# Two layers of cross-attention and expert layers on one core: stacked queries and keys kept in DRAM in the order of the tiles that load them

## The chip, the cores and the metric

One core of one Trainium2 chip. The metric is the device time of one execution in microseconds (us); the profile adds one execution recorded by the hardware. TensorE is PE in the rows (PEld its weight loads), VectorE DVE, ScalarE ACT, GpSimd POOL, and SP is the engine that does nothing here but wait and issue transfers; a row with SPq is the time that one issue took on it, not the transfer's.

## The reference, cut to what matters

Sixteen batches of 256 tokens of width 256 attend to 77 context rows each, twice, with an expert layer behind each attention. The change lies in the first attention alone, with 16 heads of 16 numbers:

```python
qh = (q @ Wq.T + bq).reshape(B, QN, H, DH).transpose(0, 2, 1, 3)
kh = (k @ Wk.T + bk).reshape(B, KN, H, DH).transpose(0, 2, 1, 3)
vh = (v @ Wv.T + bv).reshape(B, KN, H, DH).transpose(0, 2, 1, 3)
qh = layernorm(qh, q_gamma, q_beta) * scale
kh = layernorm(kh, k_gamma, k_beta)
attn = jax.nn.softmax(jnp.einsum('bhqd,bhkd->bhqk', qh, kh), axis=-1)
x = jnp.einsum('bhqk,bhkd->bhqd', attn, vh)
```

## The kernel before, in words

The program is a chain of stages with a barrier behind each: queries, keys and values of all batches (`qkv_phase`, from the start to about 151 us of the profiled span), the first attention (`attention0_phase`, about 151 to 395 us), routing and experts, the second attention, routing and experts, the last sum. Only the first two are touched.

**First stage.** A piece is two batches of keys (8 pieces, class `HeadNorm` as `k`) or 256 rows of x, which is one batch of queries (16 pieces, `q`). Each piece is projected on PE, normalised over the 16 numbers of a head on ACT and DVE, transposed on PE into one PSUM bank (`transpose`, L231), then scaled and shifted on ACT into two copies in SBUF, `full` in float32 and `high` in the rounded type float32r (`affine`, L242; the activations are L249). POOL takes `low` as the difference of the two (`part`, L252). SP stores high and low to DRAM (`store`, L258, issued at L264): a piece of keys in 2 transfers, a piece of queries in 8 of 32 rows each. Buffers of `high` and `low` are double: `affine` of piece i waits until the stores of piece i-2 have landed (L246). All engines walk through steps; SP's step (L384) loads the x rows of a later piece, stores the piece that is four steps behind, and at four steps (`PRELOAD`) loads the stacked queries and keys of batches 0 to 3. The stage ends when every engine has issued its last instruction.

**Stacked operands.** For the first attention a batch's queries and keys lie in SBUF with 96 rows: queries as high, high, low, keys as high, low, high (32 rows each, two heads of 16), so that one matmul over 96 rows gives the product to nearly full precision. The keys of a pair of heads stand in two column blocks, the other head's 16 rows being zero; POOL zeroes the four key buffers once at the start (L411). `load_queries_keys` (L283) fills them with nine transfers: three for the queries (32 rows of 8 KB each), six for the keys (16 rows of 8 runs of 308 bytes each). There are four buffers (`QK_RING`), so batch b+4 is loaded when batch b is done with.

**First attention.** It runs in half-steps u of 128 queries by 8 heads; the work of one (scores, maxima, exponentials, values, projection, layer norm, router) is spread over the 21 half-steps from u on. At half-step u: PE computes scores (L886) and DVE reduces them to maxima (L774, so that row marks the half-steps: 64 of them, u = 0 at 152.15 us); every second one the maxima are transposed, copied by ACT (L848) and sent by SP into rows 96 and 97 of the query buffer in two transfers (L679), from where the second score product (L900) takes them three half-steps later. Beside that, the first expert weights are loaded (L665, 1 MB every eight half-steps, at u = 5, 13, ...) and split into high and low in 64 chunks: ACT copies a chunk (L856), POOL subtracts (L748) into one of four tiles `low`, SP stores it (L699). SP takes all this in one program order per half-step (`half`, L672): maxima, expert weights, next batch of queries and keys (at u = 9, 13, ..., 53, after the second score product of half-step u-1), input rows, chunk of low, two result rows. At u = 12 it issues twelve loads for later stages in a row (L714, L718).

Of the kernel before, what the change touches and what calls it, by code (L numbers as in the profile page):

```python
# [12 lines left out]
ALU = mybir.AluOpType  # L13
# [151 lines left out]
class HeadNorm:  # L165
# [4 lines left out]
    def __init__(self, sb, sem, g, name, rows, w, ones, bias, gamma, beta, eps, ps_p, ps_t, parts, stored, store_rows):  # L170
# [4 lines left out]
        n = 2 * DC * rows  # L175
        at = [parts[:, i * n:(i + 1) * n] for i in range(6)]
        self.full, self.high, self.low = at[0:2], *([a.bitcast(F32R) for a in at[i:i + 2]] for i in (2, 4))
        self.stored, self.store_rows = stored, store_rows
        self.landed = 2 * len(store_rows) * 16
# [51 lines left out]
    def transpose(self, pe, i):  # L231
        p, r = i.mod(2), self.rows
        pe.wait_ge(self.s_n, i.n + 1)

        wait(pe, self.s_out, i.n)
        for a in range(2):
            for c in range(DC):
                last = pe.transpose(self.ps_t[:, (c * 2 + a) * r:(c * 2 + a + 1) * r],
                                    self.n[p][0:r, (a * DC + c) * P:(a * DC + c + 1) * P], self.g.ident[0:r, 0:r])
        last.then_inc(self.s_t, 1)  # L240

    def affine(self, act, i, s_passed):  # L242

        p, n = i.mod(2), 2 * DC * self.rows
        wait(act, self.s_low, i.shift(-1).n)
        wait(act, self.st[p], i.div(2).n * self.landed)  # L246
# [22 lines left out]
Q_ROWS = [(i * 2 * DH, (i + 1) * 2 * DH) for i in range(P // (2 * DH))]  # L269
Q_STORES = 2 * len(Q_ROWS)  # L270


def query_rows(part):

    return lambda b, first, last: part.rearrange("r b (c m) t -> m r b c t", c=DC)[first // (2 * DH)][:, b, :, :]


def key_rows(part):

    return lambda i, first, last: part.rearrange("(c p) k -> p c k", p=P)[:, :, i * 2 * LK:(i + 1) * 2 * LK]  # L280


def load_queries_keys(sp, g, b, slot):  # L283

    landed = g.s_qk[slot]
    for j, part in enumerate((0, 0, 1)):
        sp.dma_start(g.q3[slot][32 * j:32 * j + 32, :].bitcast(F32).rearrange("p (h t) -> p h t", h=HG),
                     g.q_parts[part][:, b, :, :]).then_inc(landed, 16)
    for j, part in enumerate((0, 1, 0)):
        for a in range(2):  # L290
            at = 32 * j + DH * a
            sp.dma_start(
                g.k3[slot][at:at + DH, :].bitcast(F32).rearrange("p (h a k) -> p h a k", h=HG, a=2)[:, :, a, :],
                g.k_parts[part].rearrange("(h a p) k -> a p h k", a=2, p=DH)[a][:, :, b * LK:(b + 1) * LK])\
                .then_inc(landed, 16)


def qkv_phase(nc, g):

    ctx = ExitStack()  # L300
    with ctx:
        def sb(name, shape, dt=F32):
# [10 lines left out]
        wmean, bmean = sb("wmean", [P, 2, DC * H]), sb("bmean", [2 * H, 1])  # L313
        gb, scaled, eps, bv = sb("gb", [P, 4]), sb("scaled", [P, 2]), sb("eps", [P, 1]), sb("bv", [P, 2 * D])
# [5 lines left out]
        k_split = g.w2[:, 4 * D + 12 * 2 * P:4 * D + 12 * 2 * P + 12 * 2 * LK]  # L320
# [11 lines left out]
        g.s_qk, s_neg, s_zero = [sem(f"s_qk{i}") for i in range(QK_RING)], sem("s_neg"), sem("s_zero")  # L332
        neg = g.w2[:, 6 * W2_COLS:6 * W2_COLS + HG * 2 * LK]
        ps_p, ps_t, ps_xt, ps_v = g.bank[0:4], g.bank[4], g.bank[5:7], g.bank[7]
        k = HeadNorm(sb, sem, g, "k", LK, wk, ones3, bias3[:, 0:D], gb[:, 2:3], gb[:, 3:4], eps, ps_p, ps_t,
                     k_split, [key_rows(part) for part in g.k_parts], [(0, P)])
        q = HeadNorm(sb, sem, g, "q", P, wq, ones3, bias3[:, D:2 * D], scaled[:, 0:1], scaled[:, 1:2], eps, ps_p, ps_t,
                     q_split, [query_rows(part) for part in g.q_parts], Q_ROWS)
# [24 lines left out]
        def _(sp):  # L363
            sp.dma_start(bias[:, :], g.ins["bkq"].rearrange("o (h d) -> (o h) d", d=DH)).then_inc(s_b, 16)
            sp.dma_start(wk[:, :], g.ins["wk"]).then_inc(s_wk, 16)
            for dst, src in ((wv, g.ins["wv"]), (gb, g.ins["gb"]), (bv, g.ins["bv"]), (g.ident, g.ins["ident"])):
# [17 lines left out]
            def step(s):  # L384
# [5 lines left out]
                if s.off in PRELOAD:  # L390
                    b = PRELOAD.index(s.off)
                    if b == 0:
                        sp.wait_ge(s_zero, QK_RING)
                        for st in k.st:
                            sp.wait_ge(st, NKP // 2 * k.landed)
                    sp.wait_ge(q.st[b % 2], (b // 2 + 1) * q.landed)
# [5 lines left out]
        def _(pool):  # L402
# [7 lines left out]
            for slot in range(QK_RING):  # L410
                pool.memset(g.k3[slot][0:96, :].bitcast(F32), 0.0).then_inc(s_zero, 1)  # L411
# [13 lines left out]
        def _(dve):  # L425
# [21 lines left out]
            dve.wait_ge(s_rest, 4 * 16)  # L447
            dve.tensor_scalar(scaled[:, :], gb[:, 0:2], float(DH) ** -0.5, None, ALU.mult).then_inc(s_gs, 1)
            dve.wait_ge(s_v1, 1)
# [36 lines left out]
        def _(act):  # L486
# [6 lines left out]
            act.wait_ge(s_gs, 1)  # L493
# [18 lines left out]
        def _(pe):  # L512
# [13 lines left out]
            def step(s):  # L526
# [8 lines left out]
                if (at := piece(s, 0)) is not None:  # L535
                    norm, i = at
                    if norm is k:
                        if i.off == 0:
                            pe.wait_ge(s_rest, 4 * 16)
# [25 lines left out]
def attention0_phase(nc, g):  # L565
# [3 lines left out]
    with ctx:  # L569
# [33 lines left out]
        low_st = [sem(f"low_st{i}") for i in range(4)]  # L603
# [54 lines left out]
        def _(sp):  # L658
# [12 lines left out]

            def half(u):  # L672
                m = max_rows(u)
                if m is not None:
                    sp.wait_ge(mt_out, m.n + 1)
                    b, gr = m.div(2), m.mod(2)
                    n = HG // 2 * SQ
                    for a in range(2):
# [1888 lines left out]
```

## Time and profile before

| | |
|---|---|
| median of 3 runs | 1444.58 us (1439.33 to 1449.13) |
| profiled execution | 1436.91 us, span of its instructions 1435.1 us |
| busy share of the span | PE 89%, DVE 58%, POOL 51%, ACT 45% |
| first stage | 0 to 151 us |
| first attention | 151 to about 395 us |

Read it by stages: a busy share over the whole span says little on the two stages in question. Where an engine sits idle, the row says in brackets for how long and what ended the wait. A row on transfers gives packets (the pieces into which a transfer is cut, one contiguous run each, and its small packets), bytes, and the share of 16 transfer engines' time that the packets took.

### The profile page before, as it was taken

The page shows a single profiled execution, that of the slowest core. Times are in us where ns is not written, and L with a number is a line of the kernel's source. Part 1 is how long each engine was busy: PE and PEld are TensorE (multiplying, and loading weights), DVE is VectorE, ACT ScalarE, POOL GpSimd, SP SyncE. Part 2 cuts the span into 40 slices and gives each one's busy share as a digit, 9 for nine tenths or more (in the row PEclk, how much of TensorE's full clock was granted, in tenths as well). Part 3 has the DMA queues.
Part 4 walks back from the last instruction along what each step waited for, and adds up shares of the span by engine and source line. Part 5 has one row for each costly group of instructions (what it writes and reads, how often), then busy time and mean ns, then how long its engine had stood idle before and what let it go on. Part 6 is the DMA issues. An engine that isn't in the chain of part 4 may idle for free. (4 is left out here: it accounts for less than half of the span.)

```text
span 1435.1 us, 27993 instructions
## 1 busy us (share of the span) xinstructions
PE 1270.8 (89%) x7093; PEld 995.2 (69%) x7094; DVE 838.1 (58%) x2027; ACT 648.6 (45%) x1350; POOL 728.7 (51%) x963
## 2 busy tenths in 40 slices
PE   7876779999887999999999499847999999969997
PEld 4554447667655888888888377624888888857776
DVE  5753236556584777777777588694333333346665
ACT  3544347767523545455554277635433333321110
POOL 2332236566502565555655366404655555267775
PEclk9986579999998999999999699957999999989999
DMA  3487486885352556555555588554555556774443
GB/s 105 115 197 159 132 224 193 234 216 173 123 236 87 172 156 164 165 158 171 155 170 147 183 255 226 158 234 148 174 162 161 162 161 157 136 226 131 129 134 115
DMA packets 157086, 240.44 MB, mean 168 GB/s; under 512 B 34812, under 2 KB 122125, under 8 KB 152144
## 3 DMA queue, kind: packets, MB, share of 16 engines
q1 hardware_dynamic: 134584, 173.48, 41.8%
q0 software_dynamic: 20640, 56.39, 14.1%
q10 hardware_dynamic: 1784, 9.66, 1.7%
q8 instruction: 33, 0.54, 0.2%
q14 instruction: 45, 0.37, 0.1%
HBM read 164.41 MB, written 70.55 MB: 164 GB/s over the span
## 5 line engine op out<-in xcount | busy, mean ns | idle before, releaser
L1346 POOL DMA_INDIRECT xg<-t_xn,token x160 | 151.3, 945 | 156.8 <-PE psum L2246 69.2
L2322 POOL DMA_INDIRECT su_yg<-t_y,slot x128 | 122.9, 960 | 67.5 <-issue 38.7
L2258 PE MATMUL psum<-gu,m_xT 128*128 x640 | 153.2, 383 | 0.0
L2217 DVE TENSOR_TENSOR m_h<-psum,m_sg 128x256 f32<-128x256 f32 x80 | 34.0, 425 | 158.7 <-ACT m_sg L2196 158.7
L2258 PEld LDWEIGHTS psum<-gu,m_xT 128*128 128x128 f32 x640 | 116.6, 192 | 12.9
L1599 PE MATMUL psum<-w,m_xT_high 128*128 x284 | 118.6, 418 | 0.0
L1621 PE MATMUL psum<-m_both,m_hT_high 128*128 128x512 f32 x284 | 111.3, 414 | 1.4 <-DVE top_i L1565 1.2
L1599 PE MATMUL psum<-w_low,m_xT_high 128*128 x284 | 112.3, 396 | 0.0
L1599 PE MATMUL psum<-w,m_xT_low 128*128 x284 | 112.3, 395 | 0.0
L1472 POOL DMA_INDIRECT t_y<-top_v,dest x36 | 67.7, 1880 | 69.3 <-DVE top_v L1565 66.9
L1546 DVE TENSOR_TENSOR m_both<-w,m_both 128x1024 fp32r<-128x1024 f32 x71 | 87.0, 1225 | 17.2 <-ACT m_both L1514 17.1
L1472 POOL DMA_INDIRECT t_y<-top_i,dest x35 | 62.0, 1771 | 62.8 <-DVE top_i L1565 54.6
L833 ACT ACTIVATE at_prT<-psum 77x1024 f32<-77x1024 f32 x64 | 65.3, 1020 | 60.2 <-PE psum L900 60.1
L1337 POOL DMA_INDIRECT xg<-t_xn,token x54 | 52.6, 973 | 73.0 <-POOLq L1355 51.8
L1521 ACT ACTIVATE m_h<-psum 128x512 f32<-128x512 f32 x71 | 42.4, 598 | 103.6 <-PE psum L1599 103.6
L1551 DVE TENSOR_TENSOR m_h<-psum,m_h 128x512 f32<-128x512 f32 x71 | 49.1, 691 | 61.2 <-ACT m_h L1521 61.2
L2279 PE MATMUL psum<-dn,m_hT 128*128 x320 | 82.6, 381 | 1.7 <-DVE m_y L2225 1.7
L774 DVE TENSOR_REDUCE at_mx<-psum 128x8 f32<-128x616 f32 x64 | 51.2, 800 | 51.6 <-PE psum L886 51.1
L2189 ACT ACTIVATE m_xT<-psum 128x512 f32<-128x512 f32 x80 | 47.8, 597 | 74.0 <-PE psum L2246 74.0
L1514 ACT ACTIVATE m_both<-w 128x1024 fp32r<-128x1024 f32 x71 | 74.7, 1053 | 1.6 <-PE psum L1621 1.6
L256 POOL TENSOR_TENSOR w<-w 128x512 fp32r<-128x512 f32 (+1 forms) x24 | 27.0, 1124 | 94.2 <-ACT w L249 94.2
L2021 ACT ACTIVATE sh_sg<-psum 128x512 f32<-128x512 f32 x32 | 19.1, 597 | 122.5 <-PE psum L1986 122.5
(312 smaller groups left out, 3390.1 us busy)
## 6 DMA issues: line engine op xcount, KB each, us to landing
w<-in_w SPq DMA_DIRECT2D x71, 512.0 KB, 3.8
t_y<-m_y SPq DMA_DIRECT2D x80, 256.0 KB, 2.2
q<-t_q_high SPq DMA_DIRECT2D x32, 256.0 KB, 4.2
w<-in_w SPq DMA_DIRECT2D x8, 1024.0 KB, 5.3
t_w_low<-at_low SPq DMA_DIRECT2D x64, 128.0 KB, 2.4
t_x<-at_x SPq DMA_DIRECT2D x64, 128.0 KB, 2.1
w_low<-t_w_low SPq DMA_DIRECT2D x8, 1024.0 KB, 11.8
at_yg<-t_y SPq DMA_DIRECT2D x32, 256.0 KB, 3.5
```

The lines of the kernel that those rows point to most:

```text
L774: dve.tensor_reduce(mx[m.mod(2)][:, a * HG:(a + 1) * HG].rearrange("p (c h) -> p c h", c=2), s3, AX.X, ALU.max).then_inc(mx_ready, 1)
L833: act.activation(prT[p][0:LK, :].rearrange("p (a k) -> p a k", a=2), ps_st[0:LK, :, :], ACT.Exp)\
L1337: pool.indirect_dma_start(out=g.xg0[j % GB][:, :], out_offset=None, in_=g.xn, in_offset=bass.IndirectOffsetOnAxis(ap=g.token[:, j:j + 1], ...
L1346: pool.indirect_dma_start(out=g.xg1[j % GB][:, k * D:(k + 1) * D], out_offset=None, in_=g.xn4, in_offset=bass.IndirectOffsetOnAxis(ap=g.to ...
L1472: pool.indirect_dma_start(out=g.y0, out_offset=bass.IndirectOffsetOnAxis(ap=g.dest[:, j:j + 1], axis=0), in_=y[p][:, :], in_offset=None).t ...
L1514: act.activation(part(p, 0), whole(p), ACT.Copy).then_inc(w2_high, 1)
L1546: dve.tensor_tensor(part(p, 1), whole(p), part(p, 0), ALU.subtract).then_inc(w2_low, 1)
L1599: last = pe.matmul(ps_gu[p][:, half, :], x[p][:, tile], w[:, at], start=(c == 0 and w is w13_high and x is xT_high), stop=(c == DC - 1 and ...
L1621: last = pe.matmul(ps_y[:, :], hT_high[p][:, tile], both[p][:, at:at + 2 * D], start=(c == 0), stop=(c == MC - 1))
L2258: last = pe.matmul(ps_gu[p][:, k * 2 * M1:(k + 1) * 2 * M1], xT[p][:, at:at + P], g.gu[:, bass.ds(ex[k] * (DC * 2 * M1) + c * 2 * M1, 2 * ...
L2279: last = pe.matmul(ps_y[p][:, k * D:(k + 1) * D], hT[j.mod(HELD)][:, k * P:(k + 1) * P], g.dn[:, bass.ds(ex[k] * D, D)], start=True, stop= ...
L2322: pool.indirect_dma_start(out=yg[p][k][:, :], out_offset=None, in_=g.y1, in_offset=bass.IndirectOffsetOnAxis(ap=g.slot[:, at:at + 1], axis ...
```

## The change

The scratch tensors in DRAM become `q_parts` and `k_parts` of shape (high or low, 32 rows, batch, 4, columns), so that a row of a batch is one contiguous run as the SBUF buffer has it. The zero halves of the keys are now stored too: `affine` writes a piece of keys twice, with scale and shift masked to the first and to the second head of a pair (`masked`), and the memsets on POOL go. A piece of queries is stored by two transfers, a piece of keys by four. A batch is loaded by four: the high queries into 64 rows at once from a source that is read twice, the low queries, 64 rows of keys, 32 rows of keys. The pairs of heads change their order (`pair_at`), and DVE writes the maxima in an order that lets one transfer carry them. Two chunks of low share one store (tiles: two of double width instead of four). The twelve late loads go out one per half-step, u = 12 to 23.

```diff
-            self.landed = 2 * len(store_rows) * 16
+        self.pairs, self.copies = pairs, len(gamma)
+        n = 2 * DC * rows * self.copies
...
-            last = act.activation(out[p], self.ps_t[:, 0:n], ACT.Identity, bias=self.beta, scale=self.gamma)
+            for m in range(self.copies):
+                last = act.activation(out[p].rearrange("p (n m r) -> p n m r", m=self.copies, r=r)[:, :, m, :],
+                                      self.ps_t[:, 0:2 * DC * r].rearrange("p (n r) -> p n r", r=r), ACT.Identity,
+                                      bias=self.beta[m], scale=self.gamma[m])
...
             sp.wait_ge(s_made, i.n + 1)
-            for first, last in self.store_rows:
-                sp.dma_start(self.stored[which](i.n, first, last),
-                             rows[first:last, :].bitcast(F32).rearrange("p (c t) -> p c t", c=DC)).then_inc(self.st[p], 16)
+            n = self.stored.shape[4]
+            each = rows.shape[1] // n
+            for a in range(each):
+                sp.dma_start(self.stored[which].rearrange("r b m n -> m r b n")[:, :, i.n * each + a, :],
+                             rows[:, a * n:(a + 1) * n].bitcast(F32)).then_inc(self.st[p], 16)
...
-QK_LOADS, QK_RING = 9, 4
+QK_LOADS, QK_RING = 4, 4
+Q_COLS, K_COLS = DC * SQ, DC * 2 * LK
...
 def load_queries_keys(sp, g, b, slot):
     landed = g.s_qk[slot]
-    for j, part in enumerate((0, 0, 1)):
-        sp.dma_start(g.q3[slot][32 * j:32 * j + 32, :].bitcast(F32).rearrange("p (h t) -> p h t", h=HG),
-                     g.q_parts[part][:, b, :, :]).then_inc(landed, 16)
-    for j, part in enumerate((0, 1, 0)):
-        for a in range(2):
...
+    queries, keys = (parts[:, :, b, :, :].rearrange("w r m n -> w r (m n)") for parts in (g.q_parts, g.k_parts))
+    high_twice = queries[0:1, :, :].broadcast_to([2, 2 * DH, HG * SQ])
+    for dst, src in ((g.q3[slot][0:64, :], high_twice), (g.q3[slot][64:96, :], queries[1, :, :]),
+                     (g.k3[slot][0:64, :], keys), (g.k3[slot][64:96, :], keys[0, :, :])):
+        sp.dma_start(dst.bitcast(F32), src).then_inc(landed, 16)
...
-            for slot in range(QK_RING):
-                pool.memset(g.k3[slot][0:96, :].bitcast(F32), 0.0).then_inc(s_zero, 1)
...
-        low = [sb(f"low{i}", [P, CHUNK], F32R) for i in range(4)]
+        low = [sb(f"low{i}", [P, 2 * CHUNK], F32R) for i in range(2)]
...
-                    for a in range(2):
-                        sp.dma_start(g.q3[b.mod(QK_RING)][96 + a:97 + a, gr * n:(gr + 1) * n].bitcast(F32),
-                                     mT[gr][96 + a:96 + HG:2, :].bitcast(F32)).then_inc(s_mr[gr], 16)
+                    sp.dma_start(g.q3[b.mod(QK_RING)][96:98, :].bitcast(F32)
+                                 .rearrange("p (m c t) -> p m c t", c=DC, t=SQ)[:, :, gr, :],
+                                 mT[gr][96:96 + HG, :].bitcast(F32)).then_inc(s_mr[gr], 16)
...
-                if i is not None:
+                if i is not None and i.mod(2) == 1:
                     sp.wait_ge(w_low, i.n + 1)
...
+                if 12 <= u.off < 12 + len(later):
+                    dst, src = later[u.off - 12]
+                    sp.dma_start(dst[:, :], src).then_inc(s_next, 16)
```

On SP in the first stage, one step of a piece of queries and then a batch's load stood before (a row: source line, destination and source of the transfer, the shape of its destination, and how often; `w` holds the piece, `t_q_high` and the like are the scratch tensors, `q` and `k_50` the stacked buffers):

```order
L378 DMA w<-in_x 128x2x256
L264 DMA t_q_high<-w 32x2x256 x4
L264 DMA t_q_low<-w 32x2x256 x4
L287 DMA q<-t_q_high 32x2048 x2
L287 DMA q<-t_q_low 32x2048
L292 DMA k_50<-t_k_high 16x8x77 x2
L292 DMA k_50<-t_k_low 16x8x77 x2
L292 DMA k_50<-t_k_high 16x8x77 x2
```

At the same place on SP stands now:

```order
L376 DMA w<-in_x 128x2x256
L270 DMA t_q_parts<-w 4x32x512 x2
L291 DMA q<-t_q_parts 64x1x2048
L291 DMA q<-t_q_parts 32x2048
L291 DMA k_50<-t_k_parts 64x1232
L291 DMA k_50<-t_k_parts 32x1232
```

Eight stores became two and nine loads four. The outermost dimension of a store went from 32 to 4; the first load has 64 rows as its destination, and its source (`high_twice`) is 2 copies at step 0 of 32 rows.

On SP in the first attention, half-steps 12 and 13 before, with dots for the last five late loads:

```order
L679 DMA q<-at_mT 1x4x256 x2
L661 DMA at_x_in<-in_x 128x256
L699 DMA t_w_low<-at_low 128x256
L714 DMA tri<-in_tri 128x128
L714 DMA iota<-in_iota 128x160 x2
L714 DMA not_first<-in_not_first 128x256
L714 DMA tokval<-in_tokval 128x32
L718 DMA w<-in_ctx 128x2464
L718 DMA w<-in_wk 128x512
...
L665 DMA w<-in_w 128x2048
```

The same half-steps now:

```order
L680 DMA q<-at_mT 2x4x256
L659 DMA at_x_in<-in_x 128x256
L716 DMA tri<-in_tri 128x128
L663 DMA w<-in_w 128x2048
L291 DMA q<-t_q_parts 64x1x2048
L291 DMA q<-t_q_parts 32x2048
L291 DMA k_50<-t_k_parts 64x1232
L291 DMA k_50<-t_k_parts 32x1232
L701 DMA t_w_low<-at_low 128x512
L716 DMA iota<-in_iota 128x160
```

The late loads no longer stand between one half-step's maxima and the next; the store of low stands right behind the four loads, as it stood behind the nine.

## Rows read from the trace of the kernel before

**Rows 1.** Head of the page.
```profile
span 1435.1 us, 27993 instructions
```

**Rows 2.** Stretches: length, busy PE PEld DVE ACT POOL (instructions), clock, transfer share, GB/s.
```profile
82.00:130.00 48.00, 37.30 (x136) 24.09 (x137) 22.69 (x61) 20.50 (x38) 14.27 (x20) 0.79 0.82 185
130.00:151.00 21.00, 3.43 (x16) 2.29 (x17) 3.46 (x6) 7.28 (x12) 6.30 (x6) 0.61 0.56 135
199.00:210.00 11.00, 1.67 (x12) 1.52 (x11) 0.80 (x1) 0.60 (x2) 0.49 (x1) 0.67 1.07 311
210.00:340.00 130.00, 124.86 (x1024) 88.73 (x1022) 74.94 (x217) 95.30 (x178) 82.12 (x170) 0.95 0.80 213
```

**Rows 3.** Waits between 64 and 151 us: total, times, longest.
```profile
ACT w L249 <- DMA t_q_low<-w: 31.0, 11, 6.0
```

**Rows 4.** Timeline, ACT: start, length, line; activations of the first query pieces.
```profile
64.97 1.44 ACT L249 ACTIVATE w<-psum,qkv_scaled 128x512 f32<-128x512 f32 x2 [0.68 <-PE psum L238]
...
81.75 1.45 ACT L249 ACTIVATE w<-psum,qkv_scaled 128x512 f32<-128x512 f32 x2 [0.83 <-PE psum L238]
```

**Rows 5.** Timeline, SP's issues: first batch's loads, the stage's last stores.
```profile
78.99 0.78 SPq L287 DMA_DIRECT2D q<-t_q_high  x2
...
82.16 1.34 SPq L292 DMA_DIRECT2D k<-t_k_high  x2
...
148.68 1.88 SPq L264 DMA_DIRECT2D t_q_low<-w  x4
```

**Rows 6.** Line L249, keys: nanoseconds min/median/max, first and last start.
```profile
L249 ACT ACTIVATE w<-psum,qkv_gb x16: 598/604/607, 29.7 to 62.1; 128x308 f32<-128x308 f32 x8, 128x308 fp32r<-128x308 f32 x8
```

**Rows 7.** Transfers from 34.5 to 38.5 us: the two stores of one key piece.
```profile
DMA packets 544, 0.32 MB, mean 79 GB/s; under 512 B 32, under 2 KB 544, under 8 KB 544
q1 hardware_dynamic: 544, 0.32, 25.6%
```

**Rows 8.** Transfers from 162 to 163.9 us: two transfers of maxima land.
```profile
DMA packets 16, 0.01 MB, mean 4 GB/s; under 512 B 8, under 2 KB 16, under 8 KB 16
q<-at_mT SPq DMA_DIRECT2D x2, 4.0 KB
```

**Rows 9.** Transfers from 64.3 to 66.3 us: input rows in runs of 1 KB.
```profile
DMA packets 499, 0.38 MB, mean 192 GB/s; under 512 B 23, under 2 KB 499, under 8 KB 499
q1 hardware_dynamic: 499, 0.38, 73.9%
```

**Rows 10.** Transfers from 130 to 149 us: query stores in runs of 1 KB.
```profile
DMA packets 3097, 2.56 MB, mean 135 GB/s; under 512 B 614, under 2 KB 3095, under 8 KB 3095
q1 hardware_dynamic: 3095, 2.54, 55.7%
```

**Rows 11.** Transfers from 164 to 168.5 us: expert weights in runs of 8 KB.
```profile
DMA packets 149, 1.03 MB, mean 228 GB/s; under 512 B 20, under 2 KB 24, under 8 KB 24
q1 hardware_dynamic: 149, 1.03, 65.1%
```

**Rows 12.** Busy time from 195 to 200 us, columns as in rows 2.
```profile
195.00:200.00 5.00, 4.77 (x42) 2.81 (x40) 2.74 (x8) 3.97 (x7) 1.22 (x4) 1.00 0.99 395
```

**Rows 13.** Timeline, DVE: maxima of half-steps 9, 17, 18, 32, 34, 57.
```profile
175.16 0.80 DVE L774 TENSOR_REDUCE at_mx<-psum 128x8 f32<-128x616 f32 x1 [2.93 <-PE psum L886]
199.81 0.80 DVE L774 TENSOR_REDUCE at_mx<-psum 128x8 f32<-128x616 f32 x1 [1.51 <-PE psum L886]
213.65 0.80 DVE L774 TENSOR_REDUCE at_mx<-psum 128x8 f32<-128x616 f32 x1 [0.45 <-PE psum L886]
256.39 0.80 DVE L774 TENSOR_REDUCE at_mx<-psum 128x8 f32<-128x616 f32 x1 [0.26 <-PE psum L886]
265.67 0.80 DVE L774 TENSOR_REDUCE at_mx<-psum 128x8 f32<-128x616 f32 x1 [0.24 <-PE psum L886]
341.14 0.80 DVE L774 TENSOR_REDUCE at_mx<-psum 128x8 f32<-128x616 f32 x1 [0.67 <-PE psum L886]
```

**Rows 14.** Timeline, POOL: the chunk of half-step 32.
```profile
262.43 0.72 POOL L748 TENSOR_TENSOR at_low<-w,at_high 128x256 fp32r<-128x256 f32 x1 [4.75 <-DMA t_w_low<-at_low]
```

More of the change, by code:

```diff
@@ L165, with __init__ @@
 class HeadNorm:
-    def __init__(self, sb, sem, g, name, rows, w, ones, bias, gamma, beta, eps, ps_p, ps_t, parts, stored, store_rows):
+    def __init__(self, sb, sem, g, name, rows, w, ones, bias, gamma, beta, eps, ps_p, ps_t, parts, stored, pairs):
         self.g, self.rows, self.w, self.bias, self.gamma, self.beta = g, rows, w, bias, gamma, beta
@@ L237, in transpose @@
             for c in range(DC):
-                last = pe.transpose(self.ps_t[:, (c * 2 + a) * r:(c * 2 + a + 1) * r],
+                at = (c * 2 + a if self.pairs else a * DC + c) * r
+                last = pe.transpose(self.ps_t[:, at:at + r],
                                     self.n[p][0:r, (a * DC + c) * P:(a * DC + c + 1) * P], self.g.ident[0:r, 0:r])
@@ L242, in affine @@
     def affine(self, act, i, s_passed):
-        p, n = i.mod(2), 2 * DC * self.rows
+        p, r = i.mod(2), self.rows
         wait(act, self.s_low, i.shift(-1).n)
-        wait(act, self.st[p], i.div(2).n * self.landed)
+        wait(act, self.st[p], i.div(2).n * 32 * self.copies)
         wait_alone(act, self.s_t, i.n + 1, s_passed)
         for out in (self.full, self.high):
-            last = act.activation(out[p], self.ps_t[:, 0:n], ACT.Identity, bias=self.beta, scale=self.gamma)
+            for m in range(self.copies):
+                last = act.activation(out[p].rearrange("p (n m r) -> p n m r", m=self.copies, r=r)[:, :, m, :],
+                                      self.ps_t[:, 0:2 * DC * r].rearrange("p (n r) -> p n r", r=r), ACT.Identity,
+                                      bias=self.beta[m], scale=self.gamma[m])
         last.then_inc(self.s_out, 1)
@@ L262, in store, with pair_at @@
             sp.wait_ge(s_made, i.n + 1)
-            for first, last in self.store_rows:
-                sp.dma_start(self.stored[which](i.n, first, last),
-                             rows[first:last, :].bitcast(F32).rearrange("p (c t) -> p c t", c=DC)).then_inc(self.st[p], 16)
-QK_LOADS, QK_RING = 9, 4
[L269 to L280, printed above, removed]
+            n = self.stored.shape[4]
[5 more added lines that the diff above has]
+Q_COLS, K_COLS = DC * SQ, DC * 2 * LK
+def pair_at(h):
+    return h % (HG // DC) * DC + h // (HG // DC)
 def load_queries_keys(sp, g, b, slot):
     landed = g.s_qk[slot]
-    for j, part in enumerate((0, 0, 1)):
-        sp.dma_start(g.q3[slot][32 * j:32 * j + 32, :].bitcast(F32).rearrange("p (h t) -> p h t", h=HG),
-                     g.q_parts[part][:, b, :, :]).then_inc(landed, 16)
-    for j, part in enumerate((0, 1, 0)):
-        for a in range(2):
[L291 to L295, printed above, removed]
+    queries, keys = (parts[:, :, b, :, :].rearrange("w r m n -> w r (m n)") for parts in (g.q_parts, g.k_parts))
[3 more added lines that the diff above has]
+        sp.dma_start(dst.bitcast(F32), src).then_inc(landed, 16)
 def qkv_phase(nc, g):
@@ L492, in _ @@
                 act.activation(g.k3[slot][96:98, :], neg[96:98, :], ACT.Copy)
[L493 removed]
+            act.wait_ge(s_gs, 3)
             act.wait_ge(s_half, 2)
@@ L744, in half @@
                 if i is not None:
-                    wait_alone(pool, low_st[i.mod(4)], i.div(4).n * 16, passed[1])
+                    side, half = i.mod(4) // 2, i.mod(2)
+                    if half == 0:
+                        wait_alone(pool, low_st[side], i.div(4).n * 16, passed[1])
                     pool.wait_ge(w_high, i.n + 1)
-                    pool.tensor_tensor(low[i.mod(4)][:, :], chunk(i), high[i.mod(2)][:, :], ALU.subtract).then_inc(w_low, 1)
+                    pool.tensor_tensor(low[side][:, half * CHUNK:(half + 1) * CHUNK], chunk(i), high[i.mod(2)][:, :], ALU.subtract).then_inc(w_low, 1)
                     wait_alone(pool, w_low, i.n + 1, passed[1])
@@ L2400, in __init__ @@
             scratch[n] for n in ("xn", "xn4", "y0", "y1", "beta", "w13_low"))
-        self.q_parts, self.k_parts = ([scratch[n + part] for part in ("_high", "_low")] for n in ("q", "k"))
+        self.q_parts, self.k_parts = scratch["q_parts"], scratch["k_parts"]
 def program(nc, dram_in, out, scratch):
@@ L2551 @@
         "sd": cols(a["L1_ffn_sdown_w"]),
+        "of_head": np.repeat(np.tile(np.eye(2, dtype=f), (HG // 2, 1)), DH, axis=0),
         "neg": np.stack([np.tile(np.repeat(np.arange(2) == i, LK), HG) for i in range(2)]).astype(f) * f(-1),
```

73 lines of the change are left out of this document (36 added, 37 removed).

## The prediction

> **What bounds the kernel now.** The page's head comes first: one profiled execution with a span of 1435.1 us [rows 1]; it took 1436.91 us, 1.8 more than the span, and lies 7.7 below the median of the three runs, 1444.58. The sum below is made against 1436.91, and 7.7 is added at the end. A difference of about 1% is what a measurement of this kernel can tell from none.
>
> Then the stretches [rows 2]. The first stage is not bound by an engine: from 130 to 151 us PE is busy for 3.4 us of 21. Its waits say why: ACT stood 31.0 us, 11 times, until a store of query pieces had landed [rows 3]. The first query pieces, before any such wait, came every 4.2 us (64.97 to 81.75 is four pieces) [rows 4]; from 82 us on the pace is set by SP's issues: the last four stores took 1.88 us, so eight for a piece 3.8 us, and the nine loads of a batch 4.5 us (78.99 to 83.50) [rows 5]. The last issue ends at 150.6.
>
> The first attention is bound by PE with pauses: 124.9 us busy of 130 [rows 2], about 3.0 us per half-step where nothing waits. Half-step 18 comes 13.8 us after 17, behind the twelve late loads, and 34 comes 9.3 us after 32 [rows 13]; there POOL waited 4.75 us for a store of low that stood behind expert weights and nine loads [rows 14].
>
> **What the change takes away.** SP issues for a query piece 2 stores instead of 8, for a batch 4 loads instead of 9, and half the maxima and stores of low. If the transfers ran as before, SP would no longer set the pace: 4.2 us per piece instead of an average of 5.3 would end the first stage some 22 us earlier. Against that, a key piece takes four activations instead of two, 4 x 0.60 = 2.4 us instead of 1.2 [rows 6], and POOL's subtraction doubles. While PE computes keys without a gap this is hidden; for the last three or four key pieces it is in the loop that sets the pace, some 4 us. So -18. In the attention the pauses are worth (13.8 - 3.0) at half-step 17 and some 3 us at each of three later ones, 20 us, of which I would count 17. That sum is -35. It assumes that a transfer is spread over all 16 transfer engines whatever its shape, and this is where I don't follow it.
>
> **What the change adds: narrow transfers.** The trace shows how many completions a transfer has. The two stores of a key piece, outermost dimension 128, leave 544 packets, of which 32 are small: 256 runs of data and 16 completions each [rows 7]. The two transfers of maxima, outermost dimension 4, leave 16 packets, 8 of them small: 4 runs of data and 4 completions each [rows 8]. I read a completion as one engine taking part: a transfer is dealt out along the outermost dimension of its source and destination, to as many of the 16 engines as divide both. With so few runs the maxima cannot show that their data would have needed more engines; that is the weak point. By the Trainium skill ("DMA: Bandwidth & Descriptors", "Why a DMA increments its semaphore by 16 and not by 1") the number of engines is the largest up to 16 that divides the slowest dimensions of both patterns, and its "Rules for kernel authors" say that a leading broadcast of c copies at step zero confines a transfer to c engines; 16 and 4 in the rows agree, and it speaks against this change.
>
> Read so, the new transfers stand as follows. Stores of pieces: outermost 4 in DRAM against 128 in SBUF, so 4 engines, 32 runs each. High queries into 64 rows: source 2 against 64, so 2 engines, 32 runs of 8 KB each. Maxima: 2 against 8, so 2. Low queries, keys, low, input rows: 16 as before.
>
> Time of a run on one engine: 8 KB took 0.651 x 4.5 x 16 / 125 = 0.375 us where 125 of 149 packets were such runs [rows 11]; at the best rate in the trace, 395 GB/s at a share of 0.99 [rows 12], 24.9 GB/s per engine, 0.33. I take 0.35. 1 KB took 0.739 x 2 x 16 / 476 = 0.050 us as input [rows 9] and 0.557 x 19 x 16 / 2483 = 0.068 as query store [rows 10]; 616 bytes took 0.256 x 4 x 16 / 512 = 0.032 [rows 7]. Runs of 2 KB and of 1232 bytes aren't in these rows: 2 KB lies between 0.082 (the best rate) and 0.136 (two of the slow 1 KB runs), I take 0.095; 1232 bytes between 0.050 and 0.082, I take 0.058.
>
> First stage, work of the two busiest engines: a key piece is four stores, 4 x 32 x 0.058 = 7.4 us, eight of them 59 us; a query piece 2 x 32 x 0.095 = 6.1 us, sixteen of them 98 us; twelve loads of input, 16 runs each, 10 us; a batch's load 32 x 0.35 = 11.2 and some 2 us for its other three transfers, four batches 53 us. Together 220 us, begun when the first key piece is stored, 34 us (29.7 [rows 6] plus the four activations and an issue). They hardly pause: a piece may not be rescaled before the store of the one before last has landed, so one piece is always in the queue. The stage ends with an issue, not a landing, so two query pieces (12) come off and 3.5 us for the last piece's activations, subtraction and issue go on: 34 + 220 - 12 + 3.5 = 245, against 150.6. **+94 us** (all runs at their low ends, 0.33, 0.082 and 0.050: +70; at their high ends, 0.375, 0.136 and 0.082: +162).
>
> Attention: behind the load of a batch the two engines have 13.2 us of work, and the store of low stands right behind it in their queues; 0.8 for its own runs and 1.8 that I allow for start and completion make 15.8 us from the load's issue. POOL wants that tile two half-steps later, since there are two tiles instead of four, about 8 us after the issue (half-step spacing 3.0, and 1.3 us into it: 262.43 - 4.75 against 256.39 [rows 13, 14]). It waits 7.8, and behind POOL wait ACT, whose next chunk needs this one, then the exponentials and PE. At half-step 34 a wait of 4.75 cost about 3, so 1.7 is absorbed; 6.1 is left, and a batch takes 12 + 6.1 = 18.1 us. Twelve batches, half-steps 9 to 57: 217 us, and 17 more where 1 MB of expert weights (8 runs per engine, 2.8 us) stands in front, six times: 234, against 341.14 - 175.16 = 166 [rows 13]. **+68 us** (+45 if the two engines never pause: twelve loads of 12.6 us at the low ends and some 60 us for their sixteenth of the stretch's other transfers, 212 against 166; +99 at the high ends with nothing absorbed). What this hides: the pauses above vanish into it, and the maxima, 2 engines, land within the same delay.
>
> The rest of the program is untouched. 1436.9 + 94 + 68 = 1599, plus 7.7: **1607 us**.
>
> **Rivals.** *All 16 engines after all.* Then the -35 above holds: 1402, at the runs' level **1410 us**. For it: nothing in the trace has few outer rows and many runs, so the dealing of data is not shown. Against it: four completions where 16 would be needed. It decides from the first key store: if eight key pieces come every 4.5 us, as PE lets them, this is the case.
>
> *The destination alone counts* (stores on 4 engines, loads on 16): engine work in the first stage 59 + 98 + 10 + 13 = 180, end at 205, +55; in the attention -17. 1475, at the runs' level 1483. *The source alone counts* (loads on 2, stores on 16): stores of a piece stand behind 13.2 us of load at four places, some 9.5 us lost each, 38 - 18 = +20, and +68: 1525, so 1533. The maxima before had 4 rows at the source and 4 runs in one row at the destination, so their completions don't part these.
>
> **How the numbers follow.** Narrow on both sides 0.87, all 16 engines 0.07, one side only 0.06. The narrow case alone spans 1560 (both low ends) to 1706 (both high ends); I give 1530 to 1700, which takes in the rival of 1533 and leaves out the others. Faster by over 1% 0.07, which is the case of 16 engines; within 1% 0.01; slower 0.92.
>
> **What would show it.** Right: key pieces' activations in pairs 7 to 8 us apart from the third on, ACT waiting for `t_k_parts` and `t_q_parts`; query loads landing more than 10 us after their issue instead of 4; small packets 4 per store; from 35 us to the end of the first stage a transfer share of about a quarter to a third; POOL waiting some 8 us for low once per batch. Wrong: shares near 0.8 in that stage, ACT without waits on stores, or stores of 256 KB landing in 2 to 3 us.

## The result, and the profile after

| | before | changed |
|---|---|---|
| median of 4 runs each | 1441.95 us | 1617.63 us (1615.78 to 1621.75) |
| profiled execution | 1436.91 us | 1617.56 us |
| first maxima (half-step 0) | 152.15 us | 229.77 us |
| half-steps 0 to 63 | 207.6 us | 309.2 us |

The ratio is 1.1227 with an interval of 1.1155 to 1.13: slower by 12%, 11 us above the predicted 1607. The first stage is 77.6 us longer, the attention 101.6; with 1436.91 that is 1616.1 of the 1617.56, so the rest of the program has not moved.

Transfers of the changed kernel: 2.1 us in which only stores of key pieces run (beside [rows 7]), 4.5 us of query stores, and 4 us in the attention in which only a load of high queries runs:

```profile
DMA packets 150, 0.18 MB, mean 85 GB/s; under 512 B 5, under 2 KB 150, under 8 KB 150
q1 hardware_dynamic: 150, 0.18, 26.6%
...
DMA packets 218, 0.44 MB, mean 97 GB/s; under 512 B 7, under 2 KB 7, under 8 KB 217
q1 hardware_dynamic: 217, 0.43, 26.2%
...
DMA packets 17, 0.14 MB, mean 35 GB/s; under 512 B 0, under 2 KB 0, under 8 KB 0
q1 hardware_dynamic: 17, 0.14, 13.0%
```

A share of 26.6% of 16 engines is 4.3 engines, 13.0% is 2.1: stores on four, the load on two. The first window holds 145 runs of data, 1.1 stores of 128, and 5 small packets: about 4 completions per store, where it was 16 [rows 7]. That is the number of engines which the Trainium skill ("DMA: Bandwidth & Descriptors", "Why a DMA increments its semaphore by 16 and not by 1") gives for outermost dimensions of 4 against 128, and of 2 against 64.

Stretches of the changed kernel, columns as in [rows 2]; the first two are the first stage, the third the attention:

```profile
34.00:82.00 48.00, 34.86 (x136) 21.56 (x136) 21.57 (x57) 21.43 (x45) 14.59 (x17) 0.81 0.33 104
82.00:229.00 147.00, 64.17 (x230) 41.41 (x229) 39.88 (x105) 39.46 (x70) 30.97 (x40) 0.63 0.33 109
230.00:539.00 309.00, 230.53 (x1452) 158.34 (x1453) 103.95 (x280) 136.56 (x247) 112.52 (x229) 0.69 0.47 143
```

and the attention of the kernel before as one stretch:

```profile
153.00:360.00 207.00, 190.08 (x1454) 133.84 (x1455) 103.28 (x279) 134.75 (x247) 112.76 (x229) 0.86 0.71 197
```

Two things are to be read in the last pair. PE stood still for 309 - 230.5 = 78.5 us instead of 16.9. And the same matmuls, 1452 against 1454 records, kept it busy for 230.5 us instead of 190.1, at a mean granted clock of 0.69 instead of 0.86.

Timeline of ACT in the changed kernel: the last two key pieces, then query pieces, the one at 132.40 behind a batch's load; beside [rows 4]:

```profile
71.13 2.11 ACT L251 ACTIVATE w<-psum,qkv_masked 128x308 f32<-128x308 f32 x4 [4.58 <-DMA t_k_parts<-w]
78.74 2.11 ACT L251 ACTIVATE w<-psum,qkv_masked 128x308 f32<-128x308 f32 x4 [3.94 <-DMA t_k_parts<-w]
...
106.07 1.45 ACT L251 ACTIVATE w<-psum,qkv_scaled 128x512 f32<-128x512 f32 x2 [2.77 <-DMA t_q_parts<-w]
111.91 1.45 ACT L251 ACTIVATE w<-psum,qkv_scaled 128x512 f32<-128x512 f32 x2 [2.83 <-DMA t_q_parts<-w]
132.40 1.45 ACT L251 ACTIVATE w<-psum,qkv_scaled 128x512 f32<-128x512 f32 x2 [17.32 <-DMA t_q_parts<-w]
138.20 1.45 ACT L251 ACTIVATE w<-psum,qkv_scaled 128x512 f32<-128x512 f32 x2 [2.79 <-DMA t_q_parts<-w]
```

A key piece takes 7.6 us, a query piece 5.8, one behind a load 20.5.

Waits of the attention (beside [rows 14]): total, times, longest.

```profile
POOL at_low L748 <- DMA t_w_low<-at_low: 150.5, 13, 20.3
...
PE psum L900 <- DMA q<-at_mT: 66.9, 10, 12.4
```

One of the pauses, in the timelines of SP, PE and POOL of the changed kernel: the load of a batch, the store of low behind it, the maxima behind that, the next maxima, whose issue alone took 4.89 us, and what waited.

```profile
490.06 1.02 SPq L291 DMA_DIRECT2D q<-t_q_parts  x2
...
492.31 0.42 SPq L701 DMA_DIRECT2D t_w_low<-at_low  x1
493.42 0.65 SPq L680 DMA_DIRECT2D q<-at_mT  x1
...
499.42 4.89 SPq L680 DMA_DIRECT2D q<-at_mT  x1
...
513.15 1.14 PE L900 MATMUL psum<-q,k 98*77 98x256 f32 x4 [12.41 <-DMA q<-at_mT]
...
513.24 0.73 POOL L748 TENSOR_TENSOR at_low<-w,at_high 128x256 fp32r<-128x256 f32 x1 [17.96 <-DMA t_w_low<-at_low]
```

The store of low landed 20.6 us after its own issue, 23 us after the load's first, and PE went on with the maxima of 493.42 at the same moment. The window at 13.0% above is 501 to 505 us, inside this pause: two engines at work on high queries, and the reading is that store and maxima stood behind these in their queues.

### The profile page after: what moved, and what is told of

Its sections match the earlier page's. It is cut to its first block and busy times, and to the rows that moved or that the text cites. A ratio compares the mean times of both kernels' runs of the same rounds, so it can differ in the third digit from the quotient of the medians.

```text
span 1615.6 us, 27750 instructions
## 1 busy us (share of the span) xinstructions
PE 1326.1 (82%) x7093; PEld 1027.6 (64%) x7094; DVE 837.6 (52%) x2029; ACT 659.0 (41%) x1366; POOL 732.4 (45%) x959
## 5 line engine op out<-in xcount | busy, mean ns | idle before, releaser
L748 POOL TENSOR_TENSOR at_low<-w,at_high 128x256 fp32r<-128x256 f32 x64 | 46.6, 729 | 169.3 <-DMA t_w_low<-at_low 150.5
L260 POOL TENSOR_TENSOR w<-w 128x512 fp32r<-128x512 f32 (+1 forms) x24 | 32.3, 1345 | 174.3 <-ACT w L251 174.3
L900 PE MATMUL psum<-q,k 98*77 98x256 f32 x256 | 54.0, 346 | 67.6 <-DMA q<-at_mT 66.9
L900 PEld LDWEIGHTS psum<-q,k 98*77 98x77 f32 x256 | 39.0, 191 | 70.7 <-DMA q<-at_mT 43.5
```

The source lines that it names most:

```text
L900: last = pe.matmul(ps_st[0:LK, j // 2, j % 2 * SQ:(j % 2 + 1) * SQ], g.k3[slot][0:98, (2 * h + j % 2) * LK:(2 * h + j % 2 + 1) * LK], g.q3 ...
```

## The experiments

Every one has its numbers in this table: the first maxima and the half-steps 0 to 63 by the maxima's rows, PE's busy time and mean granted clock over a stretch of the attention (its length in brackets), all from one profiled execution each, and the median of all its runs. The first and second have two runs, the fourth, eighth and eleventh one. Kernels of one group ran beside runs of the kernel before on the same chip, whose median was 1440.76 (first to fourth), 1439.65 (fifth to seventh), 1444.44 (eighth to tenth) and 1438.13 us (the last two). Each group had another chip, so across groups the ratios to these medians compare better than the totals.

| kernel | first maxima | half-steps 0 to 63 | PE busy, clock | total |
|---|---|---|---|---|
| before | 152.2 | 207.6 | 190.1 (207), 0.86 | 1441.95 |
| changed | 229.8 | 309.2 | 230.5 (309), 0.69 | 1617.63 |
| 1: stores spread | 168.6 | 293.0 | 230.1 (292), 0.72 | 1538.34 |
| 2: load spread | 196.1 | 232.2 | 215.8 (232), 0.76 | 1505.51 |
| 3: both | 133.5 | 237.9 | 220.3 (237), 0.74 | 1444.25 |
| 4: four tiles of low alone | 231.3 | 295.3 | 236.5 (294), 0.67 | 1606.85 |
| 5: 3 and 4 | 135.2 | 203.9 | 195.4 (203), 0.84 | 1418.22 |
| 6: before, two tiles of low | 150.9 | 237.4 | 218.6 (237), 0.75 | 1469.16 |
| 7: before, late loads apart | 151.9 | 210.4 | 198.5 (210), 0.83 | 1438.75 |
| 8: 5, POOL held up at 26 | 134.2 | 202.2 | 190.1 (201), 0.87 | 1411.29 |
| 9: 5, late loads together | 134.1 | 202.7 | 186.5 (202), 0.88 | 1417.77 |
| 10: 5, maxima in two | 133.2 | 223.9 | 204.2 (223), 0.80 | 1426.02 |
| 11: 5, POOL held up at 30 | 137.2 | 217.5 | 200.7 (218), 0.82 | 1434.41 |
| 12: 5, low stored first | 133.5 | 203.5 | 188.5 (202), 0.88 | 1418.42 |

**1, 2 and 3: stores spread, load spread, both.** Stores are spread by giving the scratch tensors the order (high or low, pair, row, batch, columns), in which 128 rows have one stride:

```diff
-                sp.dma_start(self.stored[which].rearrange("r b m n -> m r b n")[:, :, i.n * each + a, :],
+                sp.dma_start(self.stored[which].rearrange("m r b n -> (m r) b n")[:, i.n * each + a, :],
```

The load is spread by leaving out the double read (second experiment):

```diff
-    high_twice = queries[0:1, :, :].broadcast_to([2, 2 * DH, HG * SQ])
-    for dst, src in ((g.q3[slot][0:64, :], high_twice), (g.q3[slot][64:96, :], queries[1, :, :]),
+    for dst, src in ((g.q3[slot][0:32, :], queries[0, :, :]), (g.q3[slot][32:64, :], queries[0, :, :]),
+                     (g.q3[slot][64:96, :], queries[1, :, :]),
```

In the third the new order needs each block of 32 rows to be loaded by itself: six loads per batch, four runs to a row.

> The changed kernel with its stores spread: the scratch tensors have the four pairs outside the 32 rows, so a store's DRAM side is 128 rows at one stride, as its SBUF side is. The high queries are still loaded with a source that begins with two copies at step 0 (now one load per pair, four per batch, 64 rows of 2 KB each). Narrow transfers: engines 0 and 1 lose the stores' 146 us of runs and keep the loads; the first maxima come at 160 to 175 us instead of 229.8, half-steps 0 to 63 still take 290 to 315 us (309.2 in the changed kernel), total 1545 to 1575 us. If how a transfer is cut plays no part, and the cost is the added bytes, the doubled activations and the two tiles of low: within 1% of 1617.

> The changed kernel with the high queries loaded by two transfers of 32 rows in place of one whose source is read twice; stores with four outer rows stay. Narrow transfers: stores on four engines set the first stage's pace, keys every 7.5 us, queries every 5.5; first maxima at 190 to 205 us (229.8 in the changed kernel); the attention loses its pauses, half-steps 0 to 63 in 190 to 200 us (309.2); total 1470 to 1495. Two tiles of low alone as the cause of the pauses: half-steps 0 to 63 stay near 300 us, total over 1570. Load narrow by its destination only: no difference, 1617.

> Stores as in the first experiment, and every load of 32 rows by itself (six per batch, runs of 2 KB and 1232 bytes). Narrow transfers: the forecast's sum for 16 engines holds, first maxima at 130 to 140 us, half-steps 0 to 63 in 190 us, total 1400 to 1415, faster than the kernel before by 2%. If the bytes, the activations or the tiles cost: not under 1436.

The first stage did what was expected of it each time: 168.6, 196.1 and 133.5. Spread stores are worth 61.2 us there, a spread load 33.7, both together 96.3, so the two add up (94.9). A transfer of the same bytes in the same number of stores, cut another way, takes the stage from 229.8 to below its 152.2 of before: the cut is the cause, and not the bytes or the added activations, which are all still there. In the attention the double read is worth 77.0 us (309.2 to 232.2); in the first experiment, where it stays but comes in four loads of 2 KB runs, 16.2 us come back. That it is the number of engines shows in the third's trace too: from 39 to 42 us two key stores leave 256 runs of data and 32 small packets, so 16 completions each again, and the median key store lands in 1.9 us. The first ended 7 us under its range, with both stretches inside theirs. But the second and third missed their totals by 11 and 29 us the other way, and all of the miss is in the attention: 232 to 238 us where 190 to 200 was expected. The third's stretch and wait:

```profile
134.00:371.00 237.00, 220.28 (x1449) 151.35 (x1449) 103.26 (x279) 136.13 (x247) 112.07 (x228) 0.74 0.65 184
```

```profile
POOL at_low L748 <- DMA t_w_low<-at_low: 44.7, 8, 7.8
```

PE stands still for 16.7 us of it, as long as before; it is busy for 30 us longer, at a lower clock. POOL still waits for low, eight times, if for 7.8 us at most.

**4, 5 and 6: the two tiles of low.** The fourth undoes the pairing of the chunks in the changed kernel, the fifth in the third experiment, the sixth does the pairing alone in the kernel before. The edit, in the direction of the fourth:

```diff
-        low = [sb(f"low{i}", [P, 2 * CHUNK], F32R) for i in range(2)]
+        low = [sb(f"low{i}", [P, CHUNK], F32R) for i in range(4)]
...
-                if i is not None and i.mod(2) == 1:
+                if i is not None:
...
-                    if half == 0:
-                        wait_alone(pool, low_st[side], i.div(4).n * 16, passed[1])
+                    wait_alone(pool, low_st[i.mod(4)], i.div(4).n * 16, passed[1])
```

> The changed kernel with four tiles of low and a store per chunk, as before; nothing else undone. Narrow transfers: the first stage stays (first maxima at 229.8 us, give or take 2); a store of low may land two half-steps later before POOL waits, so the pauses shrink but the maxima still stand behind the load: half-steps 0 to 63 in 250 to 290 us instead of 309.2, total 1558 to 1598. Pairing as the whole cause: 190 to 210 us, total under 1520.

> The third experiment (stores and loads spread) with four tiles of low and a store per chunk, as before. Pairing as the cause of what was left: in the third experiment POOL still waited 45.1 us for low in the attention, up to 7.8 us at once, and PE was busy for 220 us of it instead of 190 at a mean granted clock of 0.74 instead of 0.86; with four tiles the waits go below 15 us, the clock returns to 0.85 or more, half-steps 0 to 63 take 190 to 207 us (238 in the third experiment) and the total is 1400 to 1420. Loads cut into runs of 2 KB and 1232 bytes, or the added bytes of the keys, as the cause: half-steps 0 to 63 stay at 230 to 240 us, total 1435 to 1450.

> The kernel before with one edit of the change: two tiles of low of double width, one store for two chunks. Pairing as a cause: POOL waits for low more often and longer than 28.6 us, the clock behind each pause falls, half-steps 0 to 63 take 225 to 245 us instead of 207.6, total 1455 to 1475. Pairing as harmless without narrow or finely cut transfers: within 1% of the kernel before, or up to 5 us under it, since SP issues half the stores of low.

The fourth, a single run, fell short of its range: POOL's waits for low went from 150.5 to 83.3 us, but the attention gave back only 13.9 us, since PE still waited 54.7 us for maxima that stood in the same two queues. The times of the fifth and sixth came as expected; only the fifth's waits for low, 17.5 us, and its clock, 0.84, stayed just outside what was expected (below 15, and 0.85 or more). With wide transfers four tiles are worth 26 us of the total and 34 us of the attention, and two tiles alone make the kernel before slower, ratio 1.0175 (1.0081 to 1.0268), by 29.8 us in the attention. The fifth is faster than both kernels: 1418.22 us, ratio to before 0.9846 (0.9759 to 0.9933). Its attention:

```profile
136.00:339.00 203.00, 195.41 (x1452) 136.76 (x1453) 103.63 (x278) 134.52 (x247) 112.48 (x229) 0.84 0.77 215
```

and that of the sixth:

```profile
151.00:388.00 237.00, 218.62 (x1450) 150.39 (x1451) 104.11 (x279) 135.85 (x247) 112.20 (x228) 0.75 0.61 173
```

In the sixth again PE stands still for 18.4 us, scarcely more than before's 16.9, and is busy 28.5 us longer.

**7 and 9: the late loads.** The seventh spreads them in the kernel before, the ninth puts them together again in the fifth experiment.

```diff
-                if u.loop is None and u.off == 12:
+                if u.off == 12:
...
+                if 12 <= u.off < 12 + len(later):
+                    dst, src = later[u.off - 12]
+                    sp.dma_start(dst[:, :], src).then_inc(s_next, 16)
```

> The kernel before with one edit of the change: the twelve late loads one per half-step from 12 to 23. As forecast: the 13.8 us pause at half-step 17 goes, half-steps 0 to 63 take 195 to 200 us instead of 207.6, total 1428 to 1434. If the pause only moves to the half-steps 13 to 23, where the same bytes then fall: half-steps 0 to 63 within 4 us of 207.6, total within 0.5% of the kernel before.

> The fifth experiment with the twelve late loads issued together at half-step 12, as in the kernel before. If spreading them only moves the wait, as on the kernel before (0.9979): within 0.5% of the fifth experiment's 1418 us, the pause at half-step 17 back at 10 to 14 us and the half-steps 18 to 23, which there took up to 5.9 us, at about 3. If spreading has a worth of its own once the rest is wide: 5 to 12 us longer.

No difference either way: 0.9979 (0.9945 to 1.0014) in the seventh; in the ninth, where the pause at half-step 17 is back with 15.4 us, 0.9831 (0.9779 to 0.9883) against 0.9846 (0.9759 to 0.9933) for the fifth. In the seventh the pause of 13.8 us at half-step 17 is gone; maxima of its half-steps 18, 21, 22, 25, 26, 27 and 28, beside [rows 13]:

```profile
205.42 0.80 DVE L775 TENSOR_REDUCE at_mx<-psum 128x8 f32<-128x616 f32 x1
...
214.35 0.80 DVE L775 TENSOR_REDUCE at_mx<-psum 128x8 f32<-128x616 f32 x1 [0.69 <-PE psum L887]
221.62 0.80 DVE L775 TENSOR_REDUCE at_mx<-psum 128x8 f32<-128x616 f32 x1 [0.78 <-PE psum L887]
...
230.88 0.80 DVE L775 TENSOR_REDUCE at_mx<-psum 128x8 f32<-128x616 f32 x1 [0.68 <-PE psum L887]
237.00 0.80 DVE L775 TENSOR_REDUCE at_mx<-psum 128x8 f32<-128x616 f32 x1 [1.21 <-PE psum L887]
242.88 0.80 DVE L775 TENSOR_REDUCE at_mx<-psum 128x8 f32<-128x616 f32 x1 [1.94 <-PE psum L887]
246.55 0.80 DVE L775 TENSOR_REDUCE at_mx<-psum 128x8 f32<-128x616 f32 x1 [0.17 <-PE psum L887]
```

Half-step 18 starts 8.2 us earlier than the 213.65 of before; then 7.3 us pass from 21 to 22, and 6.1 and 5.9 from 25 to 27. The wait has moved.

**8 and 11: what a pause costs.** In the fifth experiment POOL is held up by hand, by writes of a tile of its own:

```diff
+                if u.loop is None and u.off == 30:
+                    for j in range(32):
+                        pool.memset(idle[:, :], 0.0).then_inc(s_idle, 1)
+                        pool.wait_ge(s_idle, j + 1)
```

The eighth has `u.off == 26` and 16 writes.

> The fifth experiment, in whose half-steps 26 to 43 nothing waits (each 2.8 or 3.2 us at a granted clock of 1.00), with one pause made by hand: at half-step 26 POOL first writes a tile of its own 16 times, each write behind the last, about 7 us. If a pause costs only itself: PE stands some 5 us once, and the half-steps behind it take 2.8 and 3.2 us again. If the clock falls in the pause: the two half-steps behind it take about 5.9 and 4.5 us at a granted clock near 0.5, as behind the pauses of the third experiment, so that the pause costs 4 to 5 us more than PE stood still.

> As the eighth experiment, whose pause by hand fell where PE was slow already and cost nothing that shows; now 32 writes of 0.365 us, 11.7 us, at half-step 30, in a stretch where the fifth experiment ran at a granted clock of 1.00 from 222 to 240 us. If a pause costs only itself: PE stands some 8 us, and the half-steps behind it take 2.8 and 3.2 us. If the clock falls with the pause: the two half-steps behind it take about 5.9 and 3.4 to 4.5 us, the first at a clock of 0.50, 4 to 5 us beyond what PE stood still.

The eighth told nothing of the pause by hand: PE was already at the lower clock there, behind a wait of 2.61 us for maxima, and no idle time of PE follows the writes. The eleventh is clear, though a single run. Timeline of DVE, maxima of its half-steps 32 to 38:

```profile
238.81 0.80 DVE L777 TENSOR_REDUCE at_mx<-psum 128x8 f32<-128x616 f32 x1 [0.26 <-PE psum L889]
252.34 0.80 DVE L777 TENSOR_REDUCE at_mx<-psum 128x8 f32<-128x616 f32 x1 [1.93 <-PE psum L889]
257.46 0.80 DVE L777 TENSOR_REDUCE at_mx<-psum 128x8 f32<-128x616 f32 x1 [1.15 <-PE psum L889]
263.26 0.80 DVE L777 TENSOR_REDUCE at_mx<-psum 128x8 f32<-128x616 f32 x1 [1.55 <-PE psum L889]
267.92 0.80 DVE L777 TENSOR_REDUCE at_mx<-psum 128x8 f32<-128x616 f32 x1 [0.72 <-PE psum L889]
271.12 0.80 DVE L777 TENSOR_REDUCE at_mx<-psum 128x8 f32<-128x616 f32 x1 [0.68 <-PE psum L889]
273.92 0.80 DVE L777 TENSOR_REDUCE at_mx<-psum 128x8 f32<-128x616 f32 x1 [0.25 <-PE psum L889]
```

PE in the same stretch: the group of second score products before the pause, the first group behind it, and the score products again.

```profile
238.51 0.62 PE L903 MATMUL psum<-q,k 98*77 98x256 f32 x4
...
248.48 1.02 PE L942 MATMUL psum<-at_wr,at_xnT 128*128 128x8 f32 x4 [8.44 <-ACT at_xnT L873]
...
252.10 1.05 PE L903 MATMUL psum<-q,k 98*77 98x256 f32 x4
```

and its stretches, columns as in [rows 2]:

```profile
222.00:240.00 18.00, 18.00 (x157) 12.93 (x155) 11.21 (x34) 12.44 (x24) 13.35 (x35) 1.00 0.84 231
...
252.34:262.30 9.96, 9.96 (x49) 6.57 (x49) 4.17 (x13) 5.00 (x9) 6.22 (x13) 0.50 0.87 210
...
267.92:283.11 15.19, 15.15 (x133) 10.86 (x131) 9.55 (x30) 11.76 (x23) 8.94 (x19) 1.00 0.70 189
```

PE stood still for 8.44 us: it waited for ACT, and ACT for 9.69 us for POOL. From half-step 32 to 37 it took 32.3 us, where the fifth experiment needed 15.7 for them: 16.6 more. The other 8.2 us are the granted clock of 0.50 behind the pause, 1.2 GHz in place of 2.4: the same group of score products takes 1.05 us instead of 0.62, and half-steps of 5.1, 5.8 and 4.7 us go by, with PE busy without a gap, before the clock is back at 1.00. That is twice the 4 to 5 us expected.

The price does not follow the length of the pause. In the fifth experiment PE stood still for 2.34 us in half-step 17, and the next four half-steps took 20.7 us, with PE busy without a gap. The row of PE, and two of those half-steps in the columns of [rows 2]:

```profile
185.01 0.70 PE L898 MATMUL psum<-q,k 98*77 98x256 f32 x4 [2.34 <-DMA q<-at_mT]
...
189.50:194.74 5.24, 5.24 (x28) 3.19 (x28) 1.39 (x4) 2.20 (x4) 3.73 (x8) 0.50 1.09 331
...
199.78:205.66 5.88, 5.88 (x32) 4.14 (x32) 1.96 (x8) 2.19 (x4) 3.15 (x6) 0.50 0.29 91
```

In the kernel before PE stood still for four times as long in its half-step 17:

```profile
209.10 1.14 PE L900 MATMUL psum<-q,k 98*77 98x256 f32 x4 [9.33 <-DMA q<-at_mT]
```

There the clock was 0.50 up to 212.86 us only and 1.00 from 213.65 us on, and the same four half-steps took 11.6 us. What decides how long the clock stays down no run here shows.

**10 and 12: what is left in the fifth.** The tenth sends the maxima in two transfers of four rows. The twelfth issues the store of low ahead of the half-step's expert weights and batch loads.

```diff
-                    sp.dma_start(g.q3[b.mod(QK_RING)][96:98, :].bitcast(F32)
...
+                    for a in range(2):
+                        sp.dma_start(g.q3[b.mod(QK_RING)][96 + a:97 + a, :].bitcast(F32)
```

> The fifth experiment with the maxima in two transfers of four rows, on four engines instead of two. If two engines are enough for 8 runs of 1 KB once no load of 32 long runs stands on them: within 0.5% of the fifth experiment, PE waiting for maxima some 5 us in the attention in both. If they are narrow enough to matter: 5 us less or more, the wait under 2 us.

> The fifth experiment with the store of low issued ahead of the half-step's expert weights and batch loads instead of behind them. If what is left of the pauses comes from the store of low standing behind these loads: POOL's waits for it fall from 17.5 us to under 8, half-steps 18 to 22 take 3 us each instead of up to 5.9, total 1403 to 1412 us against 1418. If the maxima behind the loads hold PE as well: waits for low fall, waits for maxima (5.5 us) stay or grow, total within 0.5% of 1418.

The tenth is open: 0.9869 (0.9823 to 0.9915) against 0.9846 (0.9759 to 0.9933) for the fifth, and its profiled execution, with 1431 us the longest of its runs, has PE waiting 16.7 us for maxima instead of 5.5 and an attention 20 us longer. That wait fits neither expectation, and whether it comes of the edit or of this one execution is not shown. At least two engines are no loss that shows. The twelfth made the wait for low go altogether, and gained nothing, 0.9878 (0.983 to 0.9927). Its waits on transfers in the attention:

```profile
POOL at_xb L757 <- DMA at_x_in<-in_x: 18.0, 7, 5.1
...
PE psum L898 <- DMA q<-at_mT: 11.5, 6, 3.6
```

The wait has gone over to the input rows, which now have the store ahead of them as well, and to the maxima (5.5 us in the fifth).

## Why the prediction was right, and where its terms were not

- *Narrow transfers*: shown by the shares (4.3 and 2.1 engines) and by the first three experiments. "All 16 engines", "destination alone" and "source alone" fall: each of the two kinds of transfer costs something, and goes wide when the one outer dimension that is small is changed.
- *First stage, +94*: measured +77.6. Key pieces 7.6 us each (7.4 in the sum). The four loads of a batch, 20.5, 18.0, 17.8 and 16.7 us for the piece behind them less 5.7 for a plain one, 50.2 us (53 in the sum). The term that was too large is the query piece: 6.1 us and 10 us of input rows between them were 108 us for sixteen; a plain piece took 5.7 with its input (mean of nine, 5.1 to 6.3), so 91. The 2 KB runs cost less than the 0.095 us taken, 0.262 x 4.5 x 16 / 210 = 0.090, and what was counted as input on top was not on top.
- *Attention, +68*: measured +101.6, and this is the step that failed. The sum priced what PE stands still; that came out nearly right, 78.5 - 16.9 = 61.6 us, in part by luck: it had twelve pauses of 6.1 us, six of them 2.8 longer, and the trace has nine, of 2.3 to 13.6 us, with next to none at half-steps 29, 45 and 53. It took "half-step spacing 3.0" for every half-step that doesn't wait, those behind a pause as well. Most of these run at the lower clock: PE's busy time grew from 190.1 to 230.5 us, +40.4, which no term of the sum held. The eleventh experiment shows the mechanism by itself, 8.2 us of slow half-steps behind 8.4 us of standing, and the sixth its weight without any narrow load: PE stands still 18.4 us, 1.5 more than before, and is busy for 28.5 more.
- *The path of the wait*: low was expected 15.8 us after the load's issue, and 2.8 later where expert weights stand in front, as they do at the pause shown: 18.6. It took 23 there. The term that was too small is the 8 KB run: 17 of them in 4 us on two engines are 0.130 x 4 x 16 / 17 = 0.49 us each instead of 0.35, 4.5 us more for the load's 32. That maxima "land within the same delay" held: they come at the same moment (513.15 and 513.24), and the fourth experiment shows the price of it, for with low relieved PE waits for them still.
- *What the change takes away, -35*: half of it held. The first stage is 18.7 us shorter with wide transfers (-18), though the sum has a slip in it: sixteen pieces at 4.2 us instead of 5.3 are 17.6 us and not 22, which less 4 for the keys would have been -14. The attention's -17 rested on pauses that go, and they moved instead (seventh), while the two tiles of low cost 30 us by themselves (sixth). So the rival of 16 engines, had it been true, would have ended at 1444 and not at 1410; the 1410 needs four tiles too (fifth, 1418).
- The two errors, -16 and +34, partly cancel. The 7.7 added for the level of the runs had no counterpart either: the changed kernel's profiled execution, 1617.56, lies at its median of 1617.63, so the sum itself was 1599, 18.6 short. The total of 1607 against 1617.6 is better than its parts, and that is luck.

What stays open: why one 8 KB run took 0.49 us where nothing else moved, and 0.33 to 0.375 beside other traffic [rows 11, 12].

## What to carry to other kernels

Before merging transfers to save issues, look at the outermost dimension of source and destination: 4 in front of 32 rows is 4 engines, a source read twice is 2, and whatever is queued behind on those engines waits as well; the same bytes with 128 rows outermost cost nothing. Halving the number of buffers to halve the issues takes away the time that a store has to land, 30 us here for 32 issues. And price a pause of PE with the slow half-steps behind it, by the number of pauses and not by their length alone: here 8.2 us behind 8.4, some 9 behind 2.3 (20.7 less 11.6), and some 2 behind 9.3 (an estimate, half of the 3.8 us at 0.50).

## What was not expected of the hardware

- The clock behind a pause, above. The Trainium skill ("TensorE: Matmul & The Clock Gate", "Part 1: The HAM clock gate (the "warmup" mystery)") names the same two levels, and the eleventh experiment shows both: 1.00 in the 18 us before the pause, 0.50 in the 10 us behind it although PE is busy throughout, 1.00 again in the 15 us from 267.92 on.
- Issues on SP themselves took longer where the narrow queues were long; that the one causes the other is read from the two kernels and not shown by itself. Line of the stores in the changed kernel, nanoseconds min/median/max:

```profile
L270 SPq DMA_DIRECT2D t_k_parts<-w x32: 503/658/2073, 30.6 to 84.6; - x32
L270 SPq DMA_DIRECT2D t_q_parts<-w x32: 502/538/9792, 87.9 to 227.3; - x32
```

and in the fifth experiment, with the same stores spread:

```profile
L270 SPq DMA_DIRECT2D t_k_parts<-w x32: 319/390/1365, 31.7 to 67.5; - x32
L270 SPq DMA_DIRECT2D t_q_parts<-w x32: 319/320/467, 69.5 to 133.2; - x32
```

An issue of 9.8 us, and one of 4.9 us for maxima in the pause shown, hold up every other transfer that SP has in its order.
